# The end of a Hydra layer with features in the partitions, and the down projection over pairs of tiles, in a fused attention, FFN and Hydra kernel

## What is computed

```python
x = x + attention(layernorm(x))
x = x + ffn(layernorm(x))      # kind 1
x = x + hydra_block(layernorm(x))   # kind 2
x = x + ffn(layernorm(x))      # kind 3, same weights
```

```python
h = gelu(x @ w_down.T + b_down)          # 1024 -> 128, "down"
for _ in range(2):                        # q even, q odd
    z, xBC, dt = split(h @ in_w.T)        # 256, 256 + 16 + 16, 8
    xs, B, C = silu(causal_conv(xBC))     # 7 taps
    y = scan_forward(xs, B, C, dt) + scan_backward(xs, B, C, dt) + xs * (xs @ fcD.T + D)
    yz = y * silu(z)
    h = (yz * rsqrt(mean(yz**2, -1) + 1e-5) * norm_w) @ out_w.T
h = xmid + alpha * xmid + (1 - alpha) * h
x + h @ w_up.T + b_up                     # 128 -> 1024, "up"
```

## Time and profile before

| what | value |
|---|---|
| median of three runs | 3166.18 us (3161.08 to 3172.38) |
| the profiled execution | 3165.05 us, its span 3163.3 us |
| attention part | 0 to about 1780 us |
| PE busy | 2923.6 us, 92% |
| DVE busy | 1704.7 us, 54% |
| POOL busy | 920.7 us, 29% |
| ACT busy | 899.3 us, 28% |
| mean granted TensorE clock | 0.954 |

### The profile page before, as it was taken

The page is one execution under the profiler, slowest core; times in us unless marked ns, Lnnn a source line. Parts: engine busy times, 40 slices in busy tenths (PEclk is TensorE's granted clock), DMA queues, the critical chain, the costliest instruction groups (busy, mean ns, idle before and its releaser), DMA issues. The chain is left out here.

```text
span 3163.3 us, 42567 instructions
## 1 busy us (share of the span) xinstructions
PE 2923.6 (92%) x16896; PEld 2201.0 (70%) x16896; DVE 1704.7 (54%) x2944; ACT 899.3 (28%) x1677; POOL 920.7 (29%) x1491
## 2 busy tenths in 40 slices
...
GB/s 147 170 171 150 158 112 141 117 107 138 116 127 131 110 130 116 104 154 114 137 84 97 186 41 1 1 48 7 54 1 54 1 54 1 54 1 54 1 27 27
DMA packets 103623, 272.34 MB, mean 86 GB/s; under 512 B 12122, under 2 KB 23514, under 8 KB 101122
## 3 DMA queue, kind: packets, MB, share of 16 engines
...
q10 hardware_dynamic: 4370, 2.63, 0.3%
...
## 5 line engine op out<-in xcount | busy, mean ns | idle before, releaser
L483 DVE TENSOR_REDUCE top<-ps_attn 128x1 f32<-128x512 f32 (+3 forms) x704 | 419.9, 619 | 353.1 <-PE ps_attn L648 353.0
L394 ACT ACTIVATE pt<-ps_attn 128x512 f32<-128x512 f32 (+1 forms) x704 | 382.9, 559 | 759.0 <-PE ps_attn L675 756.4
L334 POOL TENSOR_SCALAR_AFFINE_SELECT pt<-pt 128x512 f32<-128x512 f32 x256 | 164.8, 655 | 884.2 <-ACT pt L394 881.9
L1375 PE MATMUL ps_mixer<-m_w_hi,m_xt_hi 128*128 128x512 f32 x1024 | 417.7, 408 | 2.6 <-ACT m_h_mid L1049 2.6
L1376 PE MATMUL ps_mixer<-m_w_hi,m_xt_lo 128*128 128x512 f32 x1024 | 403.1, 394 | 0.0
L1377 PE MATMUL ps_mixer<-m_w_lo,m_xt_hi 128*128 128x512 f32 x1024 | 402.9, 394 | 0.0
L645 PE MATMUL ps_attn<-k_stack,q_stack 96*128 96x512 f32 (+3 forms) x1024 | 310.4, 361 | 55.5 <-DVE top L483 47.7
L675 PE MATMUL ps_attn<-q_stack,k_stack 97*128 97x512 f32 (+3 forms) x1024 | 286.0, 339 | 13.0 <-DMA q_stack<-top_rows 11.9
L645 PEld LDWEIGHTS ps_attn<-k_stack,q_stack 96*128 96x128 f32 x1024 | 179.0, 193 | 147.7 <-DVE top L483 113.3
L1155 DVE TENSOR_TENSOR m_xt_lo<-ps_mixer,m_xt_hi 128x512 fp32r<-128x512 f32 x192 | 124.2, 686 | 265.0 <-ACT m_xt_hi L1041 265.0
L492 DVE RECIPROCAL att<-ps_attn 128x128 f32<-128x128 f32 x256 | 241.0, 943 | 18.1 <-PE ps_attn L683 18.1
...
## 6 DMA issues: line engine op xcount, KB each, us to landing
...
q_stack<-q_hi SPq DMA_DIRECT2D x128, 256.0 KB, 5.6
...
```

The source lines that it names most:

```text
L394: nc.scalar.activation(pt[k][:, heads[0]:heads[0] + len(heads), :].rearrange("p j t -> p (j t)"), ps[:, ST0 + n % 2, 0:width * len(heads)] ...
L483: nc.vector.tensor_reduce(out, ps[:, S0 + n % 2, 0:width * len(heads)].rearrange("p (j k) -> p j k", k=width), AX.X, ALU.max).then_inc(s_u ...
L1375: nc.tensor.matmul(out, a_hi, b_hi, start=first, stop=False)
```

## The change

It does six things. The products of `h_mix` swap their operands: the weights are 64 features of `x_tok`, the moving side is `mixer` (128 columns), and heads 0 and 1 (2 and 3) write the lower and upper 64 partitions of PSUM, so y has its features in the partitions. `mixer` gets four slots, and DVE makes all four tiles before it gates. z comes from two products of 512 columns in the same layout. The output projection follows at once with `yz` as weights (8 products, tokens in the partitions), the squares are summed over features by a product with a column of ones, and the norm scales the projected rows on DVE (`h_scale`), which 4 transposes turn back. `down` works on two tiles at once: `xt_hi` and `xt_lo` have three slots that lie side by side, and DOWN is bank 1. `base_b`, `up_b` and `up_t` (512 KB each) are loaded by SP behind the base weights, under a semaphore of their own. The list `ORDER` is rearranged. Smaller ones: silu in place of the convolution's buffer, and `cb_bw` written straight into `cb`.

```diff
-("up", 0), ("add_up", 0), ("turn", (2, 3)), ("moments", (3, 0)), ("up", 1), ("add_up", 1), ("norm", (3, 0)), ("down", (2, 3)),
+("up", 0), ("add_up", 0), ("turn", (2, 3)), ("moments", (3, 0)), ("up", 1), ("add_up", 1), ("norm", (3, 0)), ("down", (2, 2)),
...
-("norm", (2, 2)), ("gemm", (1, 3), 1), ("h_norm", 1), ("down", (2, 1)), ("h_back", 1), ("turn", (2, 2)), ("add", (1, 3), 1),
...
-    Y0, XT0, DOWN, UP0 = 0, 2, 0, 5
+    Y0, XT0, DOWN, UP0 = 0, 2, 1, 5
 
...
-xt_hi, xt_lo = sb("xt_hi", [P, 2, CH, P], F32R), sb("xt_lo", [P, 2, CH, P], F32R)
+xt_hi, xt_lo = sb("xt_hi", [P, CH, 3, P], F32R), sb("xt_lo", [P, CH, 3, P], F32R)
...
+x_feat, b_feat, c_feat = conv[:, 0:2, :], conv[0:DST, 2, :], sb("c_feat", [DST, COLS])
...
+z_gate, yz = (tok[:, k].rearrange("p t n -> p (t n)").rearrange("p (k n) -> p k n", k=2) for k in (1, 2))
+square, square_sum, o_tok = z_gate, z_gate[:, 0, :], tok[:, 2].rearrange("p t n -> p (t n)")[:, 0:COLS]
...
-mixer = sb("mixer", [P, 2, NH, P])
...
+mixer = sb("mixer", [P, TILES, NH, P])
...
+late = ["base_b", "up_b", "up_t"]
+PARAMS, LATE = (len(names) - len(late) + len(con) + 1) * DMA, len(late) * DMA
...
-        return turn - 1 if kind == 3 else turn if what == (2, 3) and name in ("turn", "down") else turn + 1
+        return turn - 1 if kind == 3 else turn if stage in (("turn", (2, 3)), ("down", (2, 2))) else turn + 1
...
+def turned_pair(e):
+    low, high = sorted((e % 3, (e + 1) % 3))
+    return slice(low, high + 1, high - low)
...
+        for n in late:
+            sp.dma_start(par[n][:], w[n]).then_inc(late_in, DMA)
...
-            for t in range(TILES):
-                n = TILES * q + t + 1
-                pool.wait_ge(sq_done, n)
-                nc.gpsimd.tensor_scalar(y_std[:, t:t + 1], sum_sq[:, t:t + 1], 1.0 / DIN, EPS, ALU.mult,
-                                        ALU.add).then_inc(ystd_done, 1)
-                pool.wait_ge(ystd_done, n)
-                nc.gpsimd.tensor_tensor(y_inv[:, t:t + 1], y_std[:, t:t + 1], neg_half[:, 0:1], ALU.pow).then_inc(yinv_done, 1)
+            pool.wait_ge(ystd_done, q + 1)
+            nc.gpsimd.tensor_tensor(y_inv[:, :], y_std[:, :], neg_half[:, :], ALU.pow).then_inc(yinv_done, 1)
...
+            act.wait_ge(down_ready, kind2.index(e) // 2 + 1)
+            for n in range(2):
+                place = int((e + n) % 3 > (e + 1 - n) % 3)
+                nc.scalar.activation(h_mid[:, i % 2, (t + n) * P:(t + n + 1) * P], ps[:, DOWN, place * P:(place + 1) * P], ACT.Gelu,
+                                     bias=par["down_b"][:, :]).then_inc(h_done, 1)
...
-                nc.scalar.activation(z_gate[:, 2 * k:2 * k + 2, :], ps[:, 4 + k, :].rearrange("p (t n) -> p t n", t=2),
-                                     ACT.Silu).then_inc(z_done, 1)
+                nc.scalar.activation(z_gate[:, k, :], ps[:, 4 + k, :], ACT.Silu).then_inc(z_done, 1)
...
-            for t in range(TILES):
-                act.wait_ge(yz_done, TILES * q + t + 1)
-                if t or q:
-                    act.wait_ge(sq_done, TILES * q + t)
-                nc.scalar.activation(square[:, :], yz[:, t, :], ACT.Square,
-                                     accum_out=sum_sq[:, t:t + 1]).then_inc(sq_done, 1)
-            for t in range(TILES):
-                act.wait_ge(yinv_done, TILES * q + t + 1)
-                nc.scalar.activation(yz[:, t, :], yz[:, t, :], ACT.Identity, scale=y_inv[:, t:t + 1]).then_inc(yn_done, 1)
-
-        def h_back(q):
-            for k in range(2):
-                act.wait_ge(yf_ready, 2 * q + k + 1)
-                nc.scalar.copy(yn_feat[:, k, :], ps[:, 4 + k, :]).then_inc(yf_done, 1)
+            for half in range(2):
+                cols = slice(half * 2 * P, (half + 1) * 2 * P)
+                act.wait_ge(yz_done, 2 * q + half + 1)
+                nc.scalar.activation(square[:, :, cols], yz[:, :, cols], ACT.Square).then_inc(sq_done, 1)
...
-            nc.vector.tensor_tensor(cb_bw[:, :, 0:cut], cb_ps[:, :, PB:P],
+            nc.vector.tensor_tensor(cb[:, :, 0:cut], cb_ps[:, :, PB:P],
...
+            nc.vector.tensor_copy(cb[:, :, cut:P], con["ident"][:, None, cut:P].to_broadcast([P, TILES, PB])).then_inc(cb_step, 1)
...
+            for t in range(TILES):
+                if q:
+                    dve.wait_ge(ym_ready, TILES * (q - 1) + t + 1)
...
-            mix(0)
-            for t in range(TILES):
-                if t + 1 < TILES:
-                    mix(t + 1)
-                gate(t)
+            dve.wait_ge(z_done, 2 * (q + 1))
+            for half in range(2):
+                cols = slice(half * 2 * P, (half + 1) * 2 * P)
+                dve.wait_ge(ym_ready, TILES * q + 2 * (half + 1))
+                nc.vector.tensor_tensor(yz[:, :, cols], ps[:, 6 + half, :].rearrange("p (k n) -> p k n", k=2), z_gate[:, :, cols], ALU.mult).then_inc(yz_done, 1)
...
+        def h_sum(q):
+            dve.wait_ge(sq_done, 2 * (q + 1))
+            nc.vector.tensor_tensor(square_sum, square[:, 0, :], square[:, 1, :], ALU.add).then_inc(sqsum_done, 1)
+
+        def h_back(q):
+            dve.wait_ge(ss_ready, q + 1)
+            nc.vector.tensor_scalar(y_std[:, :], ps[:, 5, 0:TILES], 1.0 / DIN, EPS, ALU.mult, ALU.add).then_inc(ystd_done, 1)
+
+        def h_scale(q):
+            dve.wait_ge(yinv_done, q + 1)
+            nc.vector.tensor_tensor(o_tok.rearrange("p (t m) -> p t m", t=TILES), ps[:, 4, :].rearrange("p (t m) -> p t m", t=TILES),
+                                    y_inv[:, :, None].to_broadcast([P, TILES, DM]), ALU.mult).then_inc(otok_done, 1)
...
-            if h == 0 and downs:
+            if h == 1 and downs:
...
-            s, n = e % 2, kind2.index(e)
-            pe.wait_ge(xlo_done, 2 * (e + 1))
-            pe.wait_ge(y_added, 2 * len([g for g in gemms if g < e]) - 1)
+            n, cols = kind2.index(e), turned_pair(e)
+            pe.wait_ge(xlo_done, 2 * (e + 2))
+            pe.wait_ge(y_added, 2 * len([g for g in gemms if g < e]))
...
-                mm = split_product(ps[:, DOWN, 0:P], wd_hi[:, k, :], wd_lo[:, k, :], xt_hi[:, s, k, :],
-                                   xt_lo[:, s, k, :], k == 0, k == CH - 1)
+                mm = split_product(ps[:, DOWN, 0:2 * P], wd_hi[:, k, :], wd_lo[:, k, :], xt_hi[:, k, cols, :],
+                                   xt_lo[:, k, cols, :], k == 0, k == CH - 1)
...
-                for t in range(2 * k, 2 * k + 2):
-                    mm = nc.tensor.matmul(ps[:, 4 + k, (t % 2) * DIN:(t % 2 + 1) * DIN], h[:, t * P:(t + 1) * P],
-                                          par["wz_t"][:, :], start=True, stop=True)
-                mm.then_inc(z_ready, 1)
+                nc.tensor.matmul(ps[:, 4 + k, :], par["wz_t"][:, k * P:(k + 1) * P], h, start=True, stop=True).then_inc(z_ready, 1)
...
-                if t >= 2:
-                    pe.wait_ge(yz_done, TILES * q + t - 1)
                 for n in range(NH):
-                    cols = slice(n * HD, (n + 1) * HD)
-                    mm = nc.tensor.matmul(ps[:, 6 + t % 2, cols], mixer[:, t % 2, n, :], x_tok[:, t, cols],
-                                          start=True, stop=True)
+                    rows = slice(n % 2 * HD, (n % 2 + 1) * HD)
+                    place = (2 * (n // 2) + t % 2) * P
+                    mm = nc.tensor.matmul(ps[rows, 6 + t // 2, place:place + P], x_tok[:, t, n * HD:(n + 1) * HD],
+                                          mixer[:, t, n, :], start=True, stop=True)
...
-            pe.wait_ge(yn_done, TILES * (q + 1))
-            for k in range(2):
-                for t in range(TILES):
-                    mm = nc.tensor.transpose(ps[:, 4 + k, t * P:(t + 1) * P], yz[:, t, k * P:(k + 1) * P], con["ident"][:, :])
-                mm.then_inc(yf_ready, 1)
+            pe.wait_ge(yz_done, 2 * (q + 1))
+            for t in range(TILES):
+                cols = slice(t * P, (t + 1) * P)
+                for k in range(2):
+                    nc.tensor.matmul(ps[:, 4, cols], yz[:, k, cols], wout[:, k, :], start=(k == 0), stop=(k == 1))
+            pe.wait_ge(sqsum_done, q + 1)
+            for t in range(TILES):
+                mm = nc.tensor.matmul(ps[:, 5, t:t + 1], square_sum[:, t * P:(t + 1) * P], ones[:, :], start=True, stop=True)
+            mm.then_inc(ss_ready, 1)
...
-            pe.wait_ge(yz_done, TILES * (q + 1))
-            for k in range(2):
-                pe.wait_ge(yf_done, 2 * q + k + 1)
-                mm = nc.tensor.matmul(ps[:, 6, :], wout[:, k, :], yn_feat[:, k, :], start=(k == 0), stop=(k == 1))
+            pe.wait_ge(otok_done, q + 1)
+            for t in range(TILES):
+                cols = slice(t * P, (t + 1) * P)
+                mm = nc.tensor.transpose(ps[:, 6, cols], o_tok[:, cols], con["ident"][:, :])
             mm.then_inc(o_ready, 1)
```

(23 more changed lines are left out.)

75 lines of the change are left out of this document (33 added, 42 removed).

## The result

| | before | after |
|---|---|---|
| median | 3163.63 us (4 runs) | 3111.19 us (3105.9 to 3116.33, 4 runs) |
| ratio | | 0.9835, 95% interval 0.982 to 0.985 |
| profiled execution, span | 3163.3 us | 3108.7 us |

What follows compares the result with a forecast made beforehand. PE was taken to set the time. Terms -38 (down pairs), -21 (mixer), -3.5 (layer's end), +32 (handover), -10 (start) and +8 (clock) sum to -32.5 us: 3134 us beside the median, range 3108 to 3160.

Steps and rivals of the forecast that it cites:

- rival 4: Handover between blocks: it doesn't wait, or the clock holds, so 32 + 8 falls to 15; 3109 us, chance 0.13.
- Down pairs, -38: Down projection: 24 products of 256 columns, 0.12 us apart, replace two sets of 2.63 us; -38 us over 16 pairs.
- Mixer, -21: Mixer products: two heads run side by side on PSUM halves and DVE sets the pace; -21 us over all layers.
- Layer's end, -3.5: End of each Hydra layer: fewer transposes and 512-column products, some small products added, root mostly hidden; -3.5 us in sum.
- Handover, +32: Between blocks: PE idles 4.1 us for DVE's chain before `turn (2,3)`, `turn (3,0)` waits about 0.5; +32 us over seven.
- The start, -10: Mixer part's start: late parameters off ACT's queue let norms finish before the basis ends; -10 us, ends 0 and -12.
- Block 0's start: From the last `gemm (1,3)` to block 0's `h_in`: 18.3 us becomes 13.2, the pairs' saving and no more.
- Clock, +8: Half of the seven handovers lose the clock for a spell, at 2.4 us each; +8 us.
- rival 2: Handovers between blocks: every one loses the clock, costing 17 us instead of 8; 3143 us, chance 0.12.

Runs made afterwards that it cites:

- experiments 3 and 4: Changed kernel with, first, four unread 512-column products filling the handover's idle time: 3105.44 us; second, DVE's handover order altered, `x_low (2,2)` made later: 3081.98 us.
- experiment 1: Changed kernel with the down projection of each pair of tiles taken back to two products of 128 columns, one tile after the other: 3201.74 us.
- the first kernel of experiment 7: Kernel with DVE's add earlier and `x_low (2,2)` later at the handover (3082 us), plus `x_low (1,0)` moved behind `h_weight` in the first layer: 3083.01 us.
- experiment 3: Changed kernel with four unread products of 512 columns on PE ahead of `turn (2,3)` at each of seven handovers: 3105.44 us.

## Why the prediction was right, and where its size was off

The sign came from the terms that the forecast named, and the runs show the large ones: the pairs, the side-by-side products, the handover's chain and the loads at the start. That 3111 is close to rival 4's 3109 is chance: its mechanism, a handover that doesn't wait, did not occur. What was mis-sized is the second layer's mixer, the handover, the layer's end and block 0's start.

- **Down pairs, -38.** The step of 0.12 us held, 24 of them in 2.97 us at 2.4 GHz (experiments 3 and 4). What the term left out is the clock: with singles in the same places the low spells of the second layer are three to four times as long, those of the handover mostly twice (experiment 1).
- **Mixer, -21.** First layer: wait and product 3.53 us against 5.21, 1.7 saved where 1.5 were forecast. Second layer: 1.9 us and no wait, against 0.8 + 2.4 forecast. The tiles came about when the forecast said: the first was to be used 7.1 us behind `turn (1,3)`, and where PE waits for it, in the first kernel of experiment 7, that is 6.9. Here the product started at 7.9, because the down pair ahead was slowed by 1.5 us, which the clock's term holds, and covered the wait. When the clock held through the pair, in three blocks of the first kernel of experiment 7, the wait was back with 0.42 us and the product at 2.3. So part of this gain is luck: one loss covers another. In each of the two layers without cover the product went from 7.1 to 3.7 us, where 2.9 was forecast. The Trainium skill, "TensorEngine Tiling (Array Packing)", Key Properties, has it that a change of tiling mode drains TensorE; the product takes 1.90 us with its changes on both sides, and the GEMM half behind it 5.58 us where it takes 5.54 elsewhere, so no run here shows more than 0.1 us.
- **A wait not counted.** In the kernel before, the GEMM half behind `turn (2,1)` waited for the gelu of a single down tile, for 0.99 us in two of the seven blocks and for 0.16 in four, where the clock had fallen ahead of it and `turn` took longer. One such wait, and the page's row of this line, whose last number is the total of such waits:

```profile
2801.61 0.47 PE L1375 MATMUL ps_mixer<-m_w_hi,m_xt_hi 128*128 128x512 f32 x1 [0.99 <-ACT m_h_mid L1049]
L1375 PE MATMUL ps_mixer<-m_w_hi,m_xt_hi 128*128 128x512 f32 x1024 | 417.7, 408 | 2.6 <-ACT m_h_mid L1049 2.6
```

In the pairs' order the gelu ends under the mixer. The prediction listed the idle times of the covered part as 1.19 and 2.04 and missed this one: 2.6 us in all.
- **Layer's end, -3.5.** The first layer's parts sum to 3.31 us (4.61 before), as forecast, and the 0.7 us of waiting at `turn (1,2)` did not come: -1.3 instead of -0.8 a block. Second layer 3.02 against 2.72: +0.3 where +0.5 stood. The one-column products take 0.10 us an instruction, 0.20 a product, near the upper bound of 0.23 taken.
- **Handover, +32.** The chain was the right one and its place too; 3.63 us instead of 4.1, and no wait at `turn (3,0)` instead of 0.5: +25. Rival 4, that it would not wait, falls.
- **The start, -10,** came to -9.5 at the delta product. **Block 0's start,** forecast at the pairs' saving, -4.8, was +4.8 instead: with the new order PE comes to these places earlier than DVE and waits 1.95 and 0.97 us ahead of two turns and 2.20 ahead of the first down pair, before the last wait of 5.58. The forecast had looked only at the stretch from the last `gemm (1,3)` on (13.2 us, measured 16.1) and at none of the three waits ahead of it. This step failed outright.
- **Clock, +8.** Seven of seven handovers lose it, as rival 2 had it, but six of them for 3.4 us and not 6.8; a second spell sits in each block in or behind the second layer's `h_cb`. 61 us against 41 make +10. That this is near +8 is partly luck. The price of 2.4 us for a fall was read from a window that cuts off the start of its spell: it began at 2641.9, not 2644, lasted 6.8 us and so cost 3.4; those at the handovers cost 1.7. And the mechanism was half right: before, too, five of the six spells began in the second layer in or behind `h_cb`, and the sixth in the first layer's, where no PE idle time stands ahead of them, and the prediction had only looked for idle times. Over the whole mixer part, from 1780 us on, the time at 1.2 GHz fell from 194 to 180 us, as the start, the first block and the last have less of it. The Trainium skill, "TensorE: Matmul & The Clock Gate", section "HAM oscillation — how this bites in real kernels", names idle gaps as the cause; experiment 3 agrees for the handover, and the falls behind `h_cb` show that gaps are not the only place.

By block this makes, against the forecast, 1.0 us less at the handover, 1.5 in the second mixer, 0.2 in the first, 0.4 for the gelu and 0.7 at the layers' ends, and 0.3 more for the clock: 3.5, where (34.4 - 7) / 7 = 3.9 were measured; the 0.4 left were not placed. Block 0's start gives back 9.6 of these 27 us.
